# Row maxima from 160-key spans with the mask added by TensorE, and a fused gate, mix and later layer norms

## What is computed

```python
h = layernorm(x) * (1 + ca) + sa
# attention block, 16 heads of 16
q, k, v = split(h @ qkv_w + qkv_b)
scores = q . k / 4, each query sees the 128 keys ahead of its own position
local  = softmax(scores) @ v
remote = latent_attention(h) @ rout_w + rout_b     # 64 pooled tokens, 4 heads of 16
gate   = sigmoid(local @ gl_w + remote @ gr_w)     # one number for each token and head
mixed  = gate * local + (1 - gate) * remote
x = x + ga * (mixed @ out_w + out_b)
# second block: its gathered attention picks 4 // 16 = 0 tokens, so a layer norm is left
h = layernorm(x) * (1 + cb) + sb
x = x + gb * (layernorm(h) * ln_g + ln_b)
```

## Time and profile before

| what | us |
|---|---|
| median of 3 runs (631.13 to 631.7) | 631.23 |
| span of the profiled execution | 629.9 |
| DVE busy | 570.6 |
| PE busy | 549.4 |
| POOL busy | 496.4 |
| ACT busy | 483.0 |

### The profile page before, as it was taken

The page is one execution under the profiler, slowest core; times in us unless marked ns, Lnnn a source line. Parts: engine busy times, 40 slices in busy tenths (PEclk is TensorE's granted clock), DMA queues, the critical chain, the costliest instruction groups (busy, mean ns, idle before and its releaser), DMA issues. The chain is left out here.

```text
span 629.9 us, 21526 instructions
## 1 busy us (share of the span) xinstructions
PE 549.4 (87%) x6447; PEld 422.1 (67%) x6447; DVE 570.6 (91%) x2318; ACT 483.0 (77%) x1062; POOL 496.4 (79%) x756
## 2 busy tenths in 40 slices
PE   2659999999979999999979999999979999999851
PEld 2257677777757677777767677777767777777630
DVE  5759999999979999999979999999979999999943
ACT  1658788888869788888878888888867888888830
POOL 3357788888868788888868788888868789888885
PEclk9969999999989999999999999999989999999975
DMA  8373000000000000000000000000000000000000
GB/s 279 117 275 130 3 2 3 10 11 10 11 15 10 11 4 9 10 11 10 11 16 10 10 10 11 11 10 3 11 15 10 10 11 10 11 10 11 10 10 17
DMA packets 12772, 18.33 MB, mean 29 GB/s; under 512 B 1925, under 2 KB 10718, under 8 KB 12510
## 3 DMA queue, kind: packets, MB, share of 16 engines
q1 hardware_dynamic: 10764, 15.43, 7.0%
q10 hardware_dynamic: 1874, 1.31, 0.8%
HBM read 12.52 MB, written 4.22 MB: 27 GB/s over the span
## 5 line engine op out<-in xcount | busy, mean ns | idle before, releaser
L1199 DVE CUSTOM_DVE_ANT_0 junk<-p_x,cst 128x256 bf16<-128x256 f32 x448 | 164.7, 413 | 0.9
L590 ACT ACTIVATE pr<-p_y 128x512 f32<-128x512 f32 x232 | 132.2, 600 | 18.7 <-PE p_y L823 17.8
L417 POOL TENSOR_TENSOR rstd<-ve,half 128x1 f32<-128x1 f32 x104 | 56.8, 555 | 47.1 <-DVE ve L1119 47.1
L407 POOL TENSOR_SCALAR_AFFINE_SELECT pr<-pr 128x512 f32<-128x512 f32 x132 | 86.7, 659 | 7.8 <-ACT pr L590 6.8
L802 PE MATMUL p_x<-kst,qst 96*128 96x128 bf16 x512 | 83.1, 220 | 0.0
L823 PE MATMUL p_y<-qst,kst 112*128 112x128 bf16 x528 | 81.2, 218 | 0.2
L411 POOL TENSOR_SCALAR_AFFINE_SELECT pr<-pr 128x512 f32<-128x512 f32 x116 | 80.8, 697 | 0.0
L822 PE MATMUL p_y<-qst,kst 112*128 112x128 bf16 x464 | 73.9, 220 | 5.0 <-DVE qst L1219 4.2
L801 PE MATMUL p_x<-kst,qst 96*128 96x128 bf16 x448 | 75.1, 221 | 1.5 <-DVE mx L1199 0.7
L581 ACT ACTIVATE qst<-p_x 96x1024 bf16<-96x1024 bf16 x66 | 67.3, 1020 | 4.4 <-PE p_x L780 2.4
L837 PE MATMUL p_pv<-pr,vp 128*18 128x128 f32 x1984 | 68.3, 278 | 1.6 <-POOL pr L411 1.6
(11 more groups left out here) (163 smaller groups left out, 1643.4 us busy)
## 6 DMA issues: line engine op xcount, KB each, us to landing
out_y<-y SPq DMA_DIRECT2D x32, 128.0 KB, 1.7
x_all<-in_x SPq DMA_DIRECT2D x1, 3072.0 KB, 17.7
pr<-in_wmod SPq DMA_DIRECT2D x1, 1024.0 KB, 10.3
cst<-in_consts SPq DMA_DIRECT2D x1, 1024.0 KB, 5.0
row<-in_rows SPq DMA_DIRECT2D x1, 816.0 KB, 7.4
x_all<-in_x SPq DMA_DIRECT2D x1, 768.0 KB, 6.7
wqk<-in_qkv_w ACTq DMA_DIRECT2D x1, 512.0 KB, 3.8
pr<-in_wmod SPq DMA_DIRECT2D x1, 512.0 KB, 5.3
```

The costliest lines, as they stand in the source:

```text
L407: ins = pool.affine_select(out=own, in_=own, compare_op=ALU.is_ge, fill=0.0, base=-1, pattern=[[0, 4], [1, P]], channel_multiplier=-1)
L590: act.activation(pr[:, 2 * i:2 * i + 2, :, :], src, ACT.Exp).then_inc(exp_done[i], 1)
L1199: ins = dve.tensor_tensor_reduce(scr, p_x[i % 2][:, at:at + 2 * P], smask, 1.0, -3.0e38, ALU.add, ALU.max, mx[:, h:h + 1])
```

## The change

The maxima. `scores` now writes six spans of three or two heads. For each span one matmul of the identity against `edge` (or `smask0` in a batch's first tile) writes the mask into the PSUM buffer; then each head takes four matmuls of 32 queries against the 160 keys that these can see, each on its own strip of 32 columns of the array, added onto the mask. `kst` becomes a ring of eight tiles with the tiles of one head side by side, so that 160 keys over a tile's edge are one run; its selector is written eight times in place of four. The maxima are one reduction for each span, negated and written into `mtok`; `negate_max` goes. PE's order takes the six spans at other places.

The gate. sigmoid(z) = (1 + tanh(z/2))/2. `wro` holds the gate's column negated as a 17th column for each head, so that the difference on POOL yields z as its 17th column; ACT takes tanh of it. DVE forms `(th + 1) * dif` and then `0.5 * that + remote`.

The norms. Both norms are two DVE instructions each; POOL's four instructions go.

```diff
+QG = P // 4
+WIN = P + QG
+S_HEADS = ((0, 3), (3, 6), (6, 9), (9, 12), (12, 14), (14, 16))
+NS = len(S_HEADS)
...
-SA_EXP, SA_QK, SA_ALL = 1, 3, 3 + RING
+SA_EXP, SA_QK, SA_ALL = 1, 3, 3 + NB
...
-        kst = sb("kst", [P, RING, H, P], BF16)
+        kst = sb("kst", [P, H, NB, P], BF16)
...
             def difference(t):
...
-                pool.tensor_tensor(heads(dif[:, :]), local[:, :, :], heads(rem[:, t[1] % RING, 0:D]), ALU.subtract)\
-                    .then_inc(dif_ready, 1)
+                pool.tensor_tensor(dif[:, :, :], local[:, :, :], rem[:, t[1] % RING, :, :], ALU.subtract).then_inc(dif_ready, 1)
...
-            act.dma_start(wro[0:LD, 0:D], rout_w).then_inc(loaded_w, 16)
+            act.dma_start(wro[0:LD, :, 0:HD], rout_w.rearrange("p (h k) -> p h k", k=HD)).then_inc(loaded_w, 16)
...
-                act.activation(ez[:, :], z[:, :], ACT.Exp, scale=-1.0).then_inc(ez_ready, 1)
+            def gate_tanh(t):
+
+                act.wait_ge(dif_ready, done(t))
+                act.wait_ge(tg_ready, done(back(t, 1)))
+                act.activation(th[:, :], dif[:, :, HD], ACT.Tanh, scale=0.5).then_inc(th_ready, 1)
...
             part1(b1)
+            for r in range(4, NB):
+                pick(r)
             act.wait_ge(su_dve, SU_ALL)
...
             def scores(t, i):
...
-                n = t[1]
-                for h in (2 * i, 2 * i + 1):
-                    at = (h % 2) * 2 * P
-                    q = qst[0:KS, n % RING, h, :]
-                    if n % NB:
-                        pe.matmul(p_x[i % 2][:, at:at + P], q, kst[0:KS, (n - 1) % RING, h, :], start=True, stop=True)
-                    ins = pe.matmul(p_x[i % 2][:, at + P:at + 2 * P], q, kst[0:KS, n % RING, h, :], start=True, stop=True)
+                n = t[1] % NB
+                h0, h1 = S_HEADS[i]
+                if n == 0:
+                    own = p_x[i % 2][:, 0:(h1 - h0) * P].rearrange("p (h n) -> p h n", n=P)
+                    pe.matmul(own, ident_bf[:, :], smask0[:, :].unsqueeze(1).to_broadcast([P, h1 - h0, P]), start=True, stop=True)
+                    for h in range(h0, h1):
+                        ins = pe.matmul(own[:, h - h0, :], qst[0:KS, t[1] % RING, h, :], kst[0:KS, h, n, :],
+                                        start=False, stop=True, skip_group_check=True)
+                else:
+                    win = p_x[i % 2][:, 0:(h1 - h0) * WIN].rearrange("p (h n) -> p h n", n=WIN)
+                    ends = win.rearrange("p h (e n) -> p h e n", n=QG)[:, :, 0:5:4, :]
+                    pe.matmul(ends, ident_bf[:, :], edge[:, :].unsqueeze(1).to_broadcast([P, h1 - h0, 2 * QG]).rearrange("p h (e n) -> p h e n", n=QG),
+                              start=True, stop=True)
+                    for h in range(h0, h1):
+                        keys = kst[0:KS, h, :, :].rearrange("p r n -> p (r n)")
+                        for g in range(4):
+                            at = n * P + g * QG - P
+                            ins = pe.matmul(win[g * QG:(g + 1) * QG, h - h0, :], qst[0:KS, t[1] % RING, h, g * QG:(g + 1) * QG],
+                                            keys[:, at:at + WIN], start=False, stop=True, skip_group_check=True,
+                                            tile_position=(0, g * QG))
                 ins.then_inc(s_psum[i], 1)
...
             def maxima(t, i):
...
-                wait_apart(dve, (s_psum[i], done(t)), (s_max[i - 2], done(t if i >= 2 else back(t, 1))),
-                           (m_ready, done(back(t, 1))))
...
-                        ins = dve.tensor_tensor_reduce(scr, p_x[i % 2][:, at:at + 2 * P], smask, 1.0, -3.0e38,
-                                                       ALU.add, ALU.max, mx[:, h:h + 1])
...
+                wait_apart(dve, (s_psum[i], done(t)), (mT_psum, done(back(t, 1))))
+                h0, h1 = S_HEADS[i]
+                w = WIN if t[1] % NB else P
+                dve.tensor_reduce(mtok[:, KS + h0:KS + h1], p_x[i % 2][:, 0:(h1 - h0) * w].rearrange("p (h n) -> p h n", n=w),
+                                  AX_X, ALU.max, negate=True).then_inc(s_max[i], 1)
...
-                dve.tensor_tensor(heads(dg[:, :]), heads(dif[:, :]), bc(gate[:, :], HD), ALU.mult).then_inc(dg_ready, 1)
+                dve.scalar_tensor_tensor(out=heads(mix[:, :]), in0=bc(th[:, :], HD), scalar=1.0, in1=dif[:, :, 0:HD],
+                                         op0=ALU.add, op1=ALU.mult).then_inc(tg_ready, 1)
...
-                dve.tensor_tensor(mix[:, :], dg[:, :], rem[:, t[1] % RING, 0:D], ALU.add).then_inc(mix_ready, 1)
+                dve.scalar_tensor_tensor(out=heads(mix[:, :]), in0=heads(mix[:, :]), scalar=0.5,
+                                         in1=rem[:, t[1] % RING, :, 0:HD], op0=ALU.mult, op1=ALU.add).then_inc(mix_ready, 1)
...
+            def scale2(t):
+
+                wait_apart(dve, (mv2_ready, done(t)), (h2_ready, done(back(t, 1))))
+                dve.scalar_tensor_tensor(out=h2a[:, :], in0=x1[:, t[1] % 2, :], scalar=mv2[:, 0:1], in1=per_batch(c1, t),
+                                         op0=ALU.subtract, op1=ALU.mult).then_inc(h2a_ready, 1)
+
+            def shift2(t):
+
+                wait_apart(dve, (rstd2_ready, done(t)), (h2a_ready, done(t)), (h3_ready, done(back(t, 1))))
+                dve.scalar_tensor_tensor(out=h2[:, :], in0=h2a[:, :], scalar=rstd2[:, :], in1=per_batch(s1, t),
+                                         op0=ALU.mult, op1=ALU.add).then_inc(h2_ready, 1)
...
             def slot(t, stages):
...
                     maxima(t, 5)
-                if C:
-                    gate_local(c)
                 if K:
                     pool_twice(k)
                 if D:
-                    norm2(d)
+                    scale2(d)
+                    shift2(d)
                 if C:
                     local_out(c)
-                    gate_sum(c)
-                if S:
-                    maxima(t, 6)
-                    maxima(t, 7)
```

More of the change, by code:

```diff
@@ L103, in build @@
         brk = sb("brk", [P, 1])
-        wro = sb("wro", [P, D + H])
+        wro = sb("wro", [P, H, HD + 1])
         wo = sb("wo", [P, (B + 1) * KC * D])
@@ L147, in build @@
         loT = sb("loT", [P, P])
-        rem = sb("rem", [P, RING, D + H])
+        rem = sb("rem", [P, RING, H, HD + 1])
         ssum = sb("ssum", [P, H])
         srec = sb("srec", [P, H])
[L151 to L158, removed]
+        local = sb("local", [P, H, HD + 1])
+        dif = sb("dif", [P, H, HD + 1])
+        th = sb("th", [P, H])
         mix = sb("mix", [P, D])
@@ L215, in build @@
         stack_copied = [counted(f"stack_copied{u}", "ACT") for u in range(4)]
-        s_psum = [counted(f"s_psum{i}", "PE") for i in range(NP)]
-        s_max = [counted(f"s_max{i}", "DVE") for i in range(NP)]
-        m_ready = counted("m_ready", "DVE")
+        s_psum = [counted(f"s_psum{i}", "PE") for i in range(NS)]
+        s_max = [counted(f"s_max{i}", "DVE") for i in range(NS)]
         mT_psum, mrow_ready, shift_ready = (counted("mT_psum", "PE", 1), counted("mrow_ready", "DVE", 1),
@@ L233, in build @@
         o_psum = counted("o_psum", "PE", 2)
[L234 to L238, removed]
+        ssum_ready, srec_ready, local_ready = (counted(n, "DVE", 2) for n in ("ssum_ready", "srec_ready", "local_ready"))
+        th_ready = counted("th_ready", "ACT", 2)
+        tg_ready, mix_ready = (counted(n, "DVE", 2) for n in ("tg_ready", "mix_ready"))
         dif_ready = counted("dif_ready", "POOL", 2)
@@ L449, in add_u @@
                 pool.tensor_tensor(ux[:, :], x1[:, t[1] % 2, :], per_batch(b3, t), ALU.add).then_inc(ux_ready, 1)
[L451 to L459, removed]
-            def scale3(t):
-                wait_apart(pool, (h3_ready, done(t)))
-                pool.tensor_tensor(ya[:, :], h3[:, :], per_batch(g3, t), ALU.mult).then_inc(ya_ready, 1)
-            def finish(t):
-                pool.wait_ge(ya_ready, done(t))
-                pool.wait_ge(ux_ready, done(t))
-                pool.wait_ge(y_stored[t[1] % 2], stored(back(t, 2)))
-                pool.tensor_tensor(y[:, t[1] % 2, :], ya[:, :], ux[:, :], ALU.add).then_inc(y_ready, 1)
             def slot(t, stages):
@@ L487, in slot @@
                     part3(k)
-                if D:
-                    scale2(d)
                 if C:
                     difference(c)
-                if D:
-                    shift2(d)
                 if T:
@@ L875, in lat_remote @@
                     pe.wait_ge(mrow_ready, done(t))
-                pe.matmul(p_qkv[:, 0:D + H], loT[:, :], wro[:, :], start=True, stop=True).then_inc(rem_psum, 1)
+                pe.matmul(p_qkv[:, 0:D + H], loT[:, :], wro[:, :, :].rearrange("p h k -> p (h k)"), start=True, stop=True).then_inc(rem_psum, 1)
             def out_tokens(t):
@@ L948, in slot @@
                 if S:
-                    scores(t, 6)
+                    scores(t, 5)
                 if T:
@@ L952, in slot @@
                     scores_t(m, 5)
```

(2 more changed lines are left out.)

171 lines of the change are left out of this document (66 added, 105 removed).

## The result

The changed kernel takes 658.57 us (median of 4 runs, 657.33 to 659.25), the one before 631.18 us in the same comparison: ratio 1.0404 (95% interval 1.0364 to 1.0444). It is 27.4 us slower. The forecast was slower by 12.2 us, 643.4 us; the time lies in the stated range (611 to 662), but above the 637 to 655 that the forecast gave for its own slots, and the loss is more than twice the forecast.

A forecast was written before the change was run, and what follows sets the result against it. The prediction took DVE to bound the kernel, with PE next. To 631.2 us it added 10.3 (plain slots) + 1 (first tiles) + 1.5 (loop jumps) + 2.9 (setup) - 3.5 (end) = +12.2: 643.4 us, range 611 to 662.

The forecast's parts named there:

- The direction and the mechanism: Slower: PE waits 1.0 us a slot before the last transposed scores, for exponentials behind a 3.46 us chain through POOL and tanh.
- Rival (a): Ahead of the last pair of transposed scores the wait does not form: faster, 610 to 625 us; chance 0.36.
- (b): On the strips, loads of weights show, a head costing 0.11 us in place of 0.07: 661 us; chance 0.07.
- (c): The four strips run one behind the other, +3.4 us a slot: near 739 us; chance 0.04 together with (d).
- (d): On ACT, tanh needs another table than the exponentials, two loads a slot: 726 us; chance 0.04 together with (c).
- Two of the signs: In the profile after: DVE busy under 500 us and waiting, and PE's busy share over 90%.
- The price of a span: On PE, mask, strips and two changes of array shape: 0.49 us for three heads, 0.40 us for two.
- So DVE sets the slot, with PE 2.2 us behind it: In a 17.02 us slot DVE does not wait, while PE is busy 14.85 us, by its 87% share of the span.
- the wait for `xn` and small waits: On PE in each slot, 0.25 us of wait for `xn` and 0.3 us of small waits remain.
- Four slots with a batch's first tile ... +1 us: In the four slots with a batch's first tile, whose scores need no strips, the change adds +1 us.
- Setup: ACT writes four more selector blocks of 1.91 us before the first slot's PE work: +2.9 us.
- the end: From the last `x1` to the end of `y`, norms without POOL instructions and a shorter gate: -3.5 us.

The follow-up runs named there:

- tanh_later: The whole change with ACT's tanh moved behind the sixth exponentials and the copy of the remote part: 629.74 us, ratio 0.995 to the kernel before.
- local_first: The whole change with DVE's division (local) moved ahead of the sixth maxima, ACT's order kept: 630.03 us, ratio 0.9948 to the kernel before.
- mask_ahead: As tanh_pooled, with the sixth span's mask matmul moved ahead of P·V's first quarter: 621.08 us, ratio 0.9777 to the kernel before.
- tanh_pooled: The whole change with the moves of both tanh_later and pooled_early: 623.17 us, ratio 0.9834 to the kernel before.
- pooled_early: The whole change with DVE's copy of the pooled tokens moved ahead of the sixth maxima: 659.36 us, ratio 1.04 to the kernel before.

## Why the prediction was right, and where it was wrong

- **The direction and the mechanism** were right. The wait stands where it was put, ahead of the last pair, put down to the exponentials, forecast 1.0 us a slot, measured 1.03. tanh_later and local_first took it away from both ends and gave 28 us each. Rival (a), that the wait doesn't form, is out. So are (b), with a head at 0.06 to 0.08 us and not 0.11; (c), with four strips in that time; and (d), since the profile after has one table load (1.28 us, in the setup) and a tanh takes 0.23 us. Two of the signs failed: DVE is busy 503.8 us (under 500 was said), and PE 86% (over 90%), since the new wait takes PE's share down.
- **The range held by luck.** What took it beyond the forecast's own 637 to 655 us was rival (b), which did not come true.
- **The price of a span** was right. Forecast 0.49 and 0.40 us; in the profile a three-head span runs from 317.43 to the next matmul at 317.92, a two-head span from 324.68 to 325.09:

```profile
317.43 0.25 PE L772 MATMUL p_x<-edge,ident_bf 128*128 128x192 bf16 x1
317.60 0.39 PE L778 MATMUL p_x<-kst,qst 96*32 96x160 bf16 x12
317.92 0.70 PE L826 MATMUL p_a<-bd,rqT 128*128 128x256 f32 x2
...
324.68 0.23 PE L772 MATMUL p_x<-edge,ident_bf 128*128 128x128 bf16 x1
```

  Twelve strip matmuls take 0.32 us and eight 0.26 with a change of shape of 0.1 in each, so a head costs 0.06 to 0.08 us. The loads of 32 columns are in the trace, 0.09 to 0.10 us long each, but those of the next head run beside the matmuls of this one and add nothing. The Trainium skill ("TensorE: Matmul & The Clock Gate", "LDWEIGHTS (loading the stationary operand)") gives a load's time by its columns, from which the prediction worked out an estimate of 0.107 us for the four loads of a head. The trace doesn't agree with that as the price of a head. That a change of shape costs 0.1 us was shown by mask_ahead (0.22 us for two).
- **The step that failed: "So DVE sets the slot, with PE 2.2 us behind it", from "PE is busy 87% of the span, so 0.872 x 17.02 = 14.85 us of a slot".** Of the 14.4 us between +12.2 and +26.6, the first tiles' slots are 8.4 and the other 28 slots 7.0; setup and end together are -1.0. The share of the whole span holds the setup and the tail, where PE is idle more than half of the time (busy 20.1 of 43.6 us and 13.6 of 34.0). The slots themselves, in the window of the earlier trace rows (length, PE busy, granted clock):

```profile
216.18:318.32 102.14, 97.07 (x1206) 1.00 0.03 10
```

  97.07 of 102.14 is 95%, 16.2 us a slot with the modelled ends, not 14.85: PE was not 2.2 us behind DVE but 0.8 by that count. Without the ends, tanh_pooled gives 16.6 us of PE's own work with the strips, where the forecast had 15.85: 0.75 us too little. The 0.55 us that it allowed for the wait for `xn` and small waits was too much, since only the wait for `pooled` is left (0.2 us shown), and so the slots of tiles four to seven came out at 17.91 us against 17.45.
- **"Four slots with a batch's first tile ... +1 us"** is the term that missed most, by 8.4 us, on the same ground: DVE had not been the bound in these slots at all. Their maxima were half as large before. The slot from 322.50 to 337.68 (15.18 us) has one wait within it, 0.36 us, and not for DVE; after, the slot from 194.14 to 211.51 (17.37 us, at the same clock) has three:

```profile
322.50 0.23 PE L811 MATMUL p_qkv<-ident_bf,mtok 128*128 128x128 bf16 x1 [2.94 <-issue]
327.72 0.41 PE L727 MATMUL p_a<-cst,xn 128*128 128x128 f32 x2 [0.36 <-ACT le L605]
```

```profile
194.14 0.23 PE L790 MATMUL p_qkv<-ident_bf,mtok 128*128 128x128 bf16 x1 [3.36 <-issue]
200.08 0.44 PE L695 MATMUL p_a<-cst,xn 128*128 128x128 f32 x2 [0.24 <-DVE xn L1109]
202.06 0.71 PE L725 MATMUL p_a<-hT,wrq 128*128 128x128 f32 x4 [0.21 <-DVE pooled L1124]
205.28 0.22 PE L801 MATMUL p_y<-qst,kst 112*128 112x128 bf16 x1 [0.99 <-ACT pr L554]
```

  So the whole new wait counted here, and so did the added masks, 384 or 256 columns wide (0.16 us for each of four, 0.12 for each of two: 0.9 us). The sum had neither of them in these slots.
- **Setup** +3.5 for +2.9, the four writes behind each other as forecast; **the end** -5.1 for -3.5, the right sign.
- **DVE**: a three-head reduction was forecast at 0.64 us, a two-head one at 0.48, and they take 0.66 and 0.49; the norm's instructions, forecast at 0.41, take 0.48 and 0.49. The groups of the reductions by line and form after:

```profile
L1171 DVE TENSOR_REDUCE mtok<-p_x 128x3 bf16<-128x480 f32 x112 | 73.7, 658 | 21.7 <-PE p_x L778 17.3 <-issue 3.7
L1171 DVE TENSOR_REDUCE mtok<-p_x 128x2 bf16<-128x320 f32 x56 | 27.5, 492 | 22.9 <-issue 20.7
```

## What to carry to other kernels

When an engine is to be relieved, take the next engine's busy share from a window of steady slots, not from the page, and do it for each kind of slot: here those in which the relieved engine was not the bound paid the whole price of the change. An instruction that now waits for another engine is dear for what is queued behind it on its own engine, and the place in the order is cheaper to change than the instruction: one move of one small ACT instruction was worth 28 us here. A wait that was taken away ahead of a longer one only lengthened that one (pooled_early), and two changes, one worth -1.6% and one +0.4% alone, made +4.0% together.

## What was not expected

The clock behind the loop's jump. PE stands for 2.9 to 3.5 us there, and the granted clock of the 4 us after it is 0.57 to 0.64 (mostly 1.2 GHz) in some turns and 1.00 (2.4 GHz) in others of the same execution. Before, in the second and third turn:

```profile
184.00:188.00 4.00, 4.00 (x15) 0.57 0.03 8
322.50:326.50 4.00, 4.00 (x33) 1.00 0.04 8
```

The slot that begins there took 16.83 us in the first of these and 15.18 in the other. After, 17.37 us at a clock of 1.00 (from 194.14) and 19.02 at 0.58 (from 338.58). One such turn at the lower clock is thus worth 1.65 us, in both kernels alike, and that makes differences of 2 us between two profiles uncertain here. The slot with the jump of the earlier trace rows, 18.65 us, is such a one at 1.00; the two other jumps before took 20.3 us by `x1`. What decides which turn gets the lower clock stays open: in the two kernels the full clock came behind stands of 2.94 and 3.36 us, the lower one behind stands of 3.04 to 3.50.
